# An attention and feed-forward kernel: VectorE adds one key's probabilities, six instead of seven quads of matmuls per group, a projection in two halves

## The chip, the cores and the metric

The kernel runs on one core of a Trainium2 chip. The metric is the device time of one execution in microseconds (us). The kernel before took 1667.95 us, the median of 3 runs (1665.87 to 1669.13).

Engines are called as the profile calls them: PE (TensorE, matmuls), PEld (TensorE's weight loads, which run ahead of the matmuls), DVE (VectorE), ACT (ScalarE), POOL (GpSimd) and SP (the queue that issues most DMAs).

## The reference, cut to what matters

The input `x` is 32 batches of 112 tokens with 512 features; `ctx` is 32 batches of 375 keys, of which the first 257 are image keys and the other 118 are text keys. The part in which the change lies is a cross-attention with 16 heads of 32 features:

```
q = rms_norm(linear(x, q_w, q_b), norm_q_w)                 # after a layer norm of x
k = rms_norm(linear(ctx_txt, k_w, k_b), norm_k_w);          v = linear(ctx_txt, v_w, v_b)
k_img = rms_norm(linear(ctx_img, k_img_w, k_img_b), ...);   v_img = linear(ctx_img, v_img_w, v_img_b)
img_x = attention(q, k_img, v_img)      # softmax over 257 keys
txt_x = attention(q, k, v)              # softmax over 118 keys
x = x + linear(txt_x + img_x, o_w, o_b)
```

After it, a router picks the 14 best tokens of each batch, which go through a second attention and a feed-forward layer. That second part is the same in both kernels.

## The kernel before, in words

A first phase projects the queries of all tokens. Then comes a loop over the 32 batches (`over_batches`: two are written out, 28 run in a hardware loop, two are written out), and then the second part of the network. Each engine has its own program, in an order written out by hand in a function `body(i, n, m, p)`. In batch `i` the engines also do the projections of batch `n = i + 1` and finish batch `p = i - 1`. Semaphores hold the engines together: `wait_ge(name, value)`.

The 376 key columns of a batch stand in three chunks. Chunk c (119 rows) holds the 118 text keys and, in its last row, the 257th image key; chunks a and b hold 128 image keys each. The 16 heads are handled in four groups `g` of four heads. For each group PE runs `scores_T(i, g)` (L1386, L1389: scores with keys on the partitions, in PSUM banks 2 to 5), ACT takes their exponentials into `prob[:, g % 2, c]` (`exps`, L729 for chunk c and L731 for a and b), POOL adds chunks a and b into `prob_img` (`sum_image`, L522), and PE runs `weighted_values(i, g)` (L1411). A *quad* there is four matmuls, one for each head, that write four different 32-partition parts of one bank. Seven quads make a group: `v_last`, `v_a`, `v_b` (the image values), `v_txt` (the text values), `ones_txt` (the text denominators), and, for the image denominators, `ones_last` (a matrix that has ones only in the 119th row) with chunk c and `ones_all` with `prob_img`. DVE then divides and adds (`normalise`: L995, L997, L1001).

What sets the order around the change:

- `scores_T(i, g)` writes over the banks that `exps(i, g - 1)` reads, so PE waits for `exp_done` ahead of it (ahead of `scores_T(i, 0)` it waits for DVE's `s_done` instead).
- There is one `prob_img`. POOL may write it for group g only when PE has read it for group g - 1 (`pv_full`).
- `values(n, 0)`, the projection of 128 image values of the next batch (12 matmuls, L1284 to L1286), stands between `weighted_values(i, 0)` and `scores_T(i, 2)`. It writes bank 0, so it waits until DVE has read there the projection of keys (`add_bias(n, 3)`, L969).
- `normalise(i, g)` reads what `weighted_values(i, g)` wrote; group g + 2 writes there again.
- `turn` (L1336) transposes the next batch's keys, after `exps(i, 3)` and `scale_k(n, 1..3)` (L975).
- DVE also ranks the router's scores (`ranks`, L1023 and L1025). PE waits for `rank_done` ahead of `weighted_values(i, 1)`.
- POOL's order in a batch is `inverse_rms` (L516) between the sums of groups 0 and 1 and of 1 and 2, and `residual` (L530, an addition of 112x512) between those of groups 2 and 3.

Of the kernel before, what the change touches and what calls it, by code (L numbers as in the profile page):

```python
# [6 lines left out]
ALU = mybir.AluOpType  # L7
# [5 lines left out]
B, L, D = 32, 112, 512  # L13
# [3 lines left out]
P = 128  # L17
# [30 lines left out]
def build(nc, t, out):  # L48
    with ExitStack() as ctx:
# [3 lines left out]
        def sem(name):  # L53
            return ctx.enter_context(nc.semaphore(name))
# [22 lines left out]
        def p1(name, shape, dt=F32):  # L77
            return phase1.enter_context(nc.sbuf_tensor(name, shape, dt))
# [53 lines left out]
        topT = [p1(f"topT{e}", [P, L], F32R) for e in range(2)]  # L132
        prob_img = p1("prob_img", [P, GH * L])
        p1("under_heads", [P, 672 + 1496 - GH * L + L])
        prob = p1("prob", [P, 2, 3, GH * L])
# [145 lines left out]
        top_full, topT_ready, pick_loaded, pick_ready = sem("top_full"), sem("topT_ready"), sem("pick_loaded"), sem("pick_ready")  # L281
        st_full, exp_done, img_summed = sem("st_full"), sem("exp_done"), sem("img_summed")
        pv_full, norm_step, pv_done = sem("pv_full"), sem("norm_step"), sem("pv_done")
# [197 lines left out]
        def _(pool):  # L481
# [36 lines left out]
            def sum_image(i, g):  # L518
                pool.wait_ge(exp_done, 8 * i + 2 * g + 2)
                if not isinstance(i, int) or i or g:  # L520
                    pool.wait_ge(pv_full, 4 * i + g)
                nc.gpsimd.tensor_tensor(prob_img[:], prob[:, g % 2, 1, :], prob[:, g % 2, 2, :], ALU.add).then_inc(img_summed, 1)  # L522

# [422 lines left out]
        def _(dve):  # L946
# [37 lines left out]
            def group_max(i, g):  # L984
# [5 lines left out]
                nc.vector.tensor_reduce(rows[:, :, 2 * g + 1], ps[0:L, 2:6, TAIL:CTX], AX.X, ALU.max).then_inc(s_done, 1)  # L990

            def normalise(i, g):
                dve.wait_ge(pv_full, 4 * i + g + 1)
# [101 lines left out]
            def body(i, n, m, p):  # L1095
# [14 lines left out]
                if n is not None:  # L1110
                    add_bias(n, 2)
                    scale_k(n, 1)
                if p is not None:
                    ranks(p)
                if n is not None:
                    add_bias(n, 3)
                    scale_k(n, 2)
                normalise(i, 0)
                if n is not None:
                    scale_k(n, 3)  # L1120
                normalise(i, 1)
                normalise(i, 2)
                if n is not None:
# [157 lines left out]
        def _(pe):  # L1281
# [56 lines left out]

            def values(n, k):

                cols, w, rows = ((slice(TXT, TXT + P), "v_img", P), (slice(TXT + P, CTXC), "v_img", P), (slice(0, TXT), "v", TXT))[k]
                full, done, bank, slot = value_slot(n, k)
                pe.wait_ge(done, slot)
                project(bank[0:rows], ctx_hi, ctx_lo, cols, w).then_inc(full, 1)

# [46 lines left out]
            def weighted_values(i, g, n):  # L1392
# [5 lines left out]
                if g >= 2:  # L1398
# [3 lines left out]
                sources = ((0, ((v_last, p_c, CHUNK_C), (v_a, p_a, P), (v_b, p_b, P))), (1, ((v_txt, p_c, CHUNK_C),)),  # L1402
                           (3, ((ones_txt, p_c, CHUNK_C),)), (2, ((ones_last, p_c, CHUNK_C), (ones_all, prob_img, P))))
                for slot, terms in sources:
                    for e, (left, right, rows) in enumerate(terms):
                        if right is prob_img:
                            pe.wait_ge(img_summed, 4 * i + g + 1)
                        for j in range(GH):
# [40 lines left out]
            def body(i, n, m, p):  # L1449
# [23 lines left out]
                if n is not None:  # L1473
                    values(n, 0)
                scores_T(i, 2)
                if p is not None:
                    pe.wait_ge(rank_done, i)
                weighted_values(i, 1, n)
                scores_T(i, 3)
                weighted_values(i, 2, n)  # L1480
                if n is not None:
# [210 lines left out]
```

## Time and profile before

| | us |
|---|---|
| median of 3 runs | 1667.95 |
| profiled execution, its time | 1665.81 |
| its span, first to last instruction | 1664.1 |
| PE busy (share of the span) | 1590.9 (96%) |
| PEld busy | 1245.3 (75%) |
| DVE busy | 1092.8 (66%) |
| ACT busy | 709.6 (43%) |
| POOL busy | 696.8 (42%) |

The mean granted TensorE clock is 0.98 of full speed. A row of the profile gives busy time, mean duration in ns, and the idle time of the engine just before the instructions with what ended it. Matmuls overlap each other, so their starts tell more than their durations: the time that a matmul takes from the next one is the distance between two starts. The loop is very regular: a batch takes 34.83 us, and its rows come again 34.83 us later with nearly the same distances.

### The profile page before, as it was taken

The numbers are of one execution on the slowest core, as the hardware profiler recorded it, in microseconds if no ns is written. First come the engines' busy times: TensorE is split into PE (matmuls) and PEld (weight loads), VectorE is DVE, ScalarE is ACT, GpSimd is POOL, SyncE is SP. The second block draws the span as 40 slices with busy tenths as digits, with TensorE's granted clock in tenths as the row PEclk, the third lists the DMA queues.
The fourth block names the chain that finished last, engine by engine and source line by source line (L and its number), as shares of the span: only waits on it lengthen the run. The fifth ranks groups of instructions, "written<-read, shape, count | busy, mean of one in ns | idle before, by whom it ended". The sixth has DMA issues, their size and how long they took to land.

```text
span 1664.1 us, 44189 instructions
## 1 busy us (share of the span) xinstructions
PE 1590.9 (96%) x17801; PEld 1245.3 (75%) x17801; DVE 1092.8 (66%) x1743; ACT 709.6 (43%) x1448; POOL 696.8 (42%) x775
## 2 busy tenths in 40 slices
PE   7999999999999999999999999999985899998997
PEld 5776777777777777777777777777763787777896
DVE  5754667776676766767667776777764675444775
ACT  5763444434444344443444434444332224555331
POOL 6761443444434444434434344343434680113542
PEclk9999999999999999999999999999996899999998
DMA  6841111121111221112211122111117205010000
GB/s 189 246 127 64 48 49 51 46 75 58 46 52 46 68 64 46 52 46 64 68 46 52 46 64 68 46 52 46 46 55 274 101 1 203 26 51 26 1 1 22
DMA packets 66152, 113.72 MB, mean 68 GB/s; under 512 B 21376, under 2 KB 36064, under 8 KB 64560
## 3 DMA queue, kind: packets, MB, share of 16 engines
q1 hardware_dynamic: 65264, 110.20, 20.8%
q0 software_dynamic: 832, 2.75, 0.6%
q8 instruction: 38, 0.62, 0.2%
q14 instruction: 18, 0.15, 0.0%
HBM read 82.59 MB, written 30.34 MB: 68 GB/s over the span
## 4 chain that ended last, share of the span: by engine, by line
PE 92%; DVE 3%; ACT 2%; issue 1%; POOL 1%; DMA 1%; DVEq 0%; ACTq 0%; POOLq 0%; SPq 0%
PE ps L1284 21%; PE ps L1286 18%; PE ps L1285 18%; PE ps L1411 11%; PE ps L1386 7%; PE ps L1336 3%; PE ps L1359 3%; PE ps L1563 2%; PE ps L1544 2%; PE ps L1389 2%; PE ps L1555 1%; PE ps L1318 1%; PE ps L1366 1%; PE ps L1299 1%; ACT q_row L688 0%
## 5 line engine op out<-in xcount | busy, mean ns | idle before, releaser
L995 DVE RECIPROCAL rec<-ps 128x224 f32<-128x224 f32 x128 | 199.2, 1556 | 96.5 <-PE ps L1411 93.7
L522 POOL TENSOR_TENSOR prob_img<-prob 128x448 f32<-128x448 f32 x128 | 157.2, 1228 | 236.0 <-PE ps L1411 214.8
L485 POOL TENSOR_TENSOR ctx_lo<-ctx_raw,ctx_hi 128x472 fp32r<-128x472 f32 x64 | 115.2, 1822 | 288.7 <-ACT ctx_hi L672 288.7
L729 ACT ACTIVATE prob<-ps 119x448 f32<-119x448 f32 x128 | 69.6, 544 | 249.4 <-PE ps L1389 249.4
L990 DVE TENSOR_REDUCE top<-ps 112x4 f32<-112x1028 f32 x128 | 156.3, 1221 | 0.0
L1386 PEld LDWEIGHTS ps<-q_all,k_all 32*128 32x128 f32 (+1 forms) x3072 | 121.6, 186 | 39.9 <-issue 31.7
L1386 PE MATMUL ps<-q_all,k_all 32*128 32x112 f32 (+1 forms) x3072 | 148.0, 300 | 1.4 <-ACT prob L731 1.4
L705 ACT ACTIVATE sq_junk<-proj 128x513 bf16<-128x513 f32 (+1 forms) x96 | 61.1, 636 | 184.6 <-DVE proj L969 184.6
L989 DVE TENSOR_REDUCE top<-ps 112x4 f32<-112x472 f32 x128 | 83.1, 649 | 84.8 <-PE ps L1359 84.8
L731 ACT ACTIVATE prob<-ps 128x896 f32<-128x896 f32 x128 | 116.8, 913 | 0.0
L1284 PE MATMUL ps<-w_v_img_hi,ctx_hi 128*128 128x512 f32 x256 | 107.6, 420 | 0.6
L1284 PE MATMUL ps<-w_k_img_hi,ctx_hi 128*128 128x512 f32 x256 | 107.5, 420 | 0.0
L1286 PE MATMUL ps<-w_v_img_hi,ctx_lo 128*128 128x512 f32 x256 | 101.3, 396 | 0.0
L1286 PE MATMUL ps<-w_k_img_hi,ctx_lo 128*128 128x512 f32 x256 | 101.1, 395 | 0.0
L1285 PE MATMUL ps<-w_k_img_lo,ctx_hi 128*128 128x512 f32 x256 | 101.0, 394 | 0.0
L1285 PE MATMUL ps<-w_v_img_lo,ctx_hi 128*128 128x512 f32 x256 | 100.8, 394 | 0.0
L1286 PE MATMUL ps<-hT_hi,ring_lo 128*128 128x448 f32 x224 | 83.0, 371 | 0.0
L1389 PE MATMUL ps<-topT,pick_img 32*128 32x112 f32 x1024 | 80.8, 296 | 0.0
L516 POOL TENSOR_TENSOR rstd<-sq_sum,neg_half 128x1 f32<-128x1 f32 x96 | 52.6, 548 | 56.4 <-ACT sq_junk L705 56.4
L642 POOL TENSOR_TENSOR ring_lo<-ring,wo_hi 128x512 fp32r<-128x512 f32 x16 | 20.6, 1291 | 128.2 <-ACT wo_hi L886 128.2
L1023 DVE SCALAR_TENSOR_TENSOR equal<-ps,score_now,later 112x112 f32<-112x112 f32 x32 | 10.8, 337 | 92.5 <-PE ps L1371 92.5
L1218 DVE TENSOR_REDUCE neg_top<-ps 112x1 f32<-112x112 f32 (+1 forms) x64 | 28.4, 446 | 57.9 <-PE ps L1545 57.9
(320 smaller groups left out, 4491.2 us busy)
## 6 DMA issues: line engine op xcount, KB each, us to landing
ctx_raw<-in_ctx_dram SPq DMA_DIRECT2D x32, 748.0 KB, 4.2
xh_dram<-xh SPq DMA_DIRECT2D x32, 448.0 KB, 3.1
q_dram<-q_turned SPq DMA_DIRECT2D x28, 256.0 KB, 2.8
q_all<-q_dram SPq DMA_DIRECT2D x32, 224.0 KB, 3.1
xh<-in_x_dram SPq DMA_DIRECT2D x32, 224.0 KB, 2.8
out_dram<-out_sb SPq DMA_DIRECT2D x32, 224.0 KB, 2.3
xa<-in_x_dram SPq DMA_DIRECT2D x21, 256.0 KB, 3.4
ring<-in_wq_dram SPq DMA_DIRECT2D x1, 4096.0 KB, 13.8
```

The costliest lines, as they stand in the source:

```text
L485: nc.gpsimd.tensor_tensor(ctx_lo[:, :, cols], ctx_raw[:, :, cols], ctx_hi[:, :, cols].bitcast(F32), ALU.subtract).then_inc(ctx_lo_done, 1)
L522: nc.gpsimd.tensor_tensor(prob_img[:], prob[:, g % 2, 1, :], prob[:, g % 2, 2, :], ALU.add).then_inc(img_summed, 1)
L731: nc.scalar.activation(prob[:, g % 2, 1:3, :].rearrange("p c (j q) -> p j c q", j=GH), ps[:, 2:6, L:3 * L].rearrange("p j (c q) -> p j c q ...
L989: nc.vector.tensor_reduce(rows[:, :, 2 * g], ps[0:L, 2:6, 0:TXT], AX.X, ALU.max)
L990: nc.vector.tensor_reduce(rows[:, :, 2 * g + 1], ps[0:L, 2:6, TAIL:CTX], AX.X, ALU.max).then_inc(s_done, 1)
L995: nc.vector.reciprocal(rec[:], bank[:, 2:4]).then_inc(norm_step, 1)
L1284: nc.tensor.matmul(o_, a_hi, b_hi, start=start, stop=False)
L1285: nc.tensor.matmul(o_, a_hi, b_lo, start=False, stop=False)
L1286: return nc.tensor.matmul(o_, a_lo, b_hi, start=False, stop=stop)
L1386: nc.tensor.matmul(ps[0:rows, 2 + j, out_cols], k_all[head, g, cols], q_all[head, g, :], start=True, stop=False)
L1389: last = nc.tensor.matmul(ps[0:rows, 2 + j, out_cols], pick[head, g, :], topT[g // 2][head, :], start=False, stop=True)
L1411: last = nc.tensor.matmul(ps[HD * j:HD * (j + 1), bank, slot * L:(slot + 1) * L], left[0:rows, cols], right[0:rows, L * j:L * (j + 1)], st ...
```

## The change

It does the following:

- A fourth step is put between ACT's exponentials and the image denominators. `add_tail(i, g)` on DVE waits for POOL's sum (`img_summed`) and adds `prob` of chunk c, times `ones_last`, to `prob_img` on partitions 96 to 118. `ones_last` is zero on 96 to 117 and one on 118, so only the 257th image key's row is added.
- The quad `ones_last` with chunk c is gone. The quad `ones_all` with `prob_img` now waits for `tail_added` instead of `img_summed`.
- `prob_img` has two buffers, `prob_img[:, g % 2]`. POOL's sum for group g now waits until `weighted_values` of group g - 2 is done, not g - 1. The memory comes out of the unused tile `under_heads`.
- `values(n, 0)` is cut into two halves of 6 matmuls. The first stays where it was, the second stands between `scores_T(i, 3)` and `weighted_values(i, 2)`.
- On DVE, `add_bias(n, 3)` and `scale_k(n, 2)` stand ahead of `ranks(p)` instead of behind it. `add_tail(i, 0)` stands ahead of `ranks(p)`, `add_tail(i, 1)` behind `normalise(i, 0)`, and `add_tail(i, 2)` and `add_tail(i, 3)` both behind `normalise(i, 1)`, ahead of `normalise(i, 2)`.

```diff
@@ POOL
             def sum_image(i, g):
                 pool.wait_ge(exp_done, 8 * i + 2 * g + 2)
-                if not isinstance(i, int) or i or g:
-                    pool.wait_ge(pv_full, 4 * i + g)
-                nc.gpsimd.tensor_tensor(prob_img[:], prob[:, g % 2, 1, :], prob[:, g % 2, 2, :], ALU.add).then_inc(img_summed, 1)
+                if not isinstance(i, int) or i or g >= 2:
+                    pool.wait_ge(pv_full, 4 * i + g - 1)
+                nc.gpsimd.tensor_tensor(prob_img[:, g % 2], prob[:, g % 2, 1, :], prob[:, g % 2, 2, :], ALU.add).then_inc(img_summed, 1)
@@ DVE
+            def add_tail(i, g):
+                dve.wait_ge(img_summed, 4 * i + g + 1)
+                last_rows = slice(P - HD, CHUNK_C)
+                nc.vector.scalar_tensor_tensor(prob_img[last_rows, g % 2], prob[last_rows, g % 2, 0, :], ones_last[last_rows, 0:1],
+                                               prob_img[last_rows, g % 2], ALU.mult, ALU.add).then_inc(tail_added, 1)
...
+                if n is not None:
+                    add_bias(n, 3)
+                    scale_k(n, 2)
+                add_tail(i, 0)
                 if p is not None:
                     ranks(p)
-                if n is not None:
-                    add_bias(n, 3)
-                    scale_k(n, 2)
                 normalise(i, 0)
+                add_tail(i, 1)
                 if n is not None:
                     scale_k(n, 3)
                 normalise(i, 1)
+                add_tail(i, 2)
+                add_tail(i, 3)
                 normalise(i, 2)
@@ PE
-            def values(n, k):
+            def values(n, k, chunks=range(KC)):
...
-                           (3, ((ones_txt, p_c, CHUNK_C),)), (2, ((ones_last, p_c, CHUNK_C), (ones_all, prob_img, P))))
+                           (3, ((ones_txt, p_c, CHUNK_C),)), (2, ((ones_all, prob_img[:, g % 2], P),)))
...
-                        if right is prob_img:
-                            pe.wait_ge(img_summed, 4 * i + g + 1)
+                        if slot == 2:
+                            pe.wait_ge(tail_added, 4 * i + g + 1)
...
                 weighted_values(i, 0, n)
                 if n is not None:
-                    values(n, 0)
+                    values(n, 0, range(0, 2))
                 scores_T(i, 2)
...
                 weighted_values(i, 1, n)
                 scores_T(i, 3)
+                if n is not None:
+                    values(n, 0, range(2, 4))
                 weighted_values(i, 2, n)
```

The changed file has other line numbers: L1294 to L1296 are the projections' matmuls, L1399 and L1402 the scores, L1424 the weighted values and L1346 the transposes; on DVE, L995 is `add_tail`, L1001 to L1007 `normalise` and L1029 and L1031 `ranks`.

On PE, at the end of `scores_T(i, 3)` and through `weighted_values(i, 2)` in the loop, the order before was:

```order
L1386 MATMUL ps<-q_all,k_all 128x112 x4
L1389 MATMUL ps<-topT,pick_img 128x112 x4
L1411 MATMUL ps<-prob,v_last 32x112 x4
L1411 MATMUL ps<-prob,v_a 32x112 x4
L1411 MATMUL ps<-prob,v_b 32x112 x4
L1411 MATMUL ps<-prob,v_txt 32x112 x4
L1411 MATMUL ps<-prob,ones_txt 32x112 x4
L1411 MATMUL ps<-prob,ones_last 32x112 x4
L1411 MATMUL ps<-prob_img,ones_all 32x112 x4
L1336 MATMUL ps<-ident,proj 128x118 x4
```

Now it is this, from the last three of the six projection matmuls that stand between the scores and the values:

```order
L1294 MATMUL ps<-w_v_img_hi,ctx_hi 128x512
L1295 MATMUL ps<-w_v_img_lo,ctx_hi 128x512
L1296 MATMUL ps<-w_v_img_hi,ctx_lo 128x512
L1424 MATMUL ps<-prob,v_last 32x112 x4
L1424 MATMUL ps<-prob,v_a 32x112 x4
L1424 MATMUL ps<-prob,v_b 32x112 x4
L1424 MATMUL ps<-prob,v_txt 32x112 x4
L1424 MATMUL ps<-prob,ones_txt 32x112 x4
L1424 MATMUL ps<-prob_img,ones_all 32x112 x4
L1346 MATMUL ps<-ident,proj 128x118 x4
```

Half of the projection moved in ahead of the group, and one quad of the group is gone.

On DVE, from `scale_k(n, 1)` to the start of `normalise(i, 0)` in the loop, the order before was:

```order
L975 SCALAR_TENSOR_TENSOR proj<-proj,rstd,w_txt 118x512
L1023 SCALAR_TENSOR_TENSOR equal<-ps,score_now,later 112x112
L1025 ISA
L1025 SCALAR_TENSOR_TENSOR equal,rank<-ps,score_now,equal 112x112
L968 REGISTER_ALU
L969 TENSOR_TENSOR proj<-ps,ki_bias 128x512
L974 REGISTER_ALU
L975 SCALAR_TENSOR_TENSOR proj<-proj,rstd,w_img 128x512
L995 RECIPROCAL rec<-ps 128x224
```

Now it is:

```order
L975 SCALAR_TENSOR_TENSOR proj<-proj,rstd,w_txt 118x512
L968 REGISTER_ALU
L969 TENSOR_TENSOR proj<-ps,ki_bias 128x512
L974 REGISTER_ALU
L975 SCALAR_TENSOR_TENSOR proj<-proj,rstd,w_img 128x512
L995 SCALAR_TENSOR_TENSOR prob_img<-prob,ones_last,prob_img 23x448
L1029 SCALAR_TENSOR_TENSOR equal<-ps,score_now,later 112x112
L1031 ISA
L1031 SCALAR_TENSOR_TENSOR equal,rank<-ps,score_now,equal 112x112
L1001 RECIPROCAL rec<-ps 128x224
```

The bias and the scaling of the last keys moved ahead of the ranking, and the first tail stands between them.

Later on DVE, from `normalise(i, 1)` to the start of `normalise(i, 2)`, the order before was:

```order
L995 RECIPROCAL rec<-ps 128x224
L996 REGISTER_ALU
L997 TENSOR_TENSOR o_two<-ps,rec 128x224
L998 REGISTER_ALU
L1001 TENSOR_TENSOR o_space<-o_two 128x112
L995 RECIPROCAL rec<-ps 128x224
```

Now it is:

```order
L1001 RECIPROCAL rec<-ps 128x224
L1002 REGISTER_ALU
L1003 TENSOR_TENSOR o_two<-ps,rec 128x224
L1004 REGISTER_ALU
L1007 TENSOR_TENSOR o_space<-o_two 128x112
L995 SCALAR_TENSOR_TENSOR prob_img<-prob,ones_last,prob_img 23x448 x2
L1001 RECIPROCAL rec<-ps 128x224
```

The tails of groups 2 and 3 stand there one behind the other, ahead of the next division.

## Rows read from the trace of the kernel before

**Rows 1.** The page's busy times of the engines, and the chain that ended last.

```profile
PE 1590.9 (96%) x17801; PEld 1245.3 (75%) x17801; DVE 1092.8 (66%) x1743; ACT 709.6 (43%) x1448; POOL 696.8 (42%) x775
...
PE 92%; DVE 3%; ACT 2%; issue 1%; POOL 1%; DMA 1%; DVEq 0%; ACTq 0%; POOLq 0%; SPq 0%
```

**Rows 2.** Windows: one batch, and most of the loop; the clock follows POOL.

```profile
810.00:844.83 34.83, 34.77 (x485) 26.72 (x484) 24.52 (x38) 14.89 (x30) 14.38 (x15) 1.00 0.18 55
240.00:1200.00 960.00, 958.42 (x13369) 736.82 (x13362) 676.34 (x1023) 412.37 (x803) 393.65 (x410) 1.00 0.18 54
```

**Rows 3.** Timeline of PEld in one batch: start, duration, what [idle before].

```profile
831.26 0.16 PEld L1411 LDWEIGHTS ps<-prob,v_last 119*32 119x32 f32 x8
...
832.84 0.19 PEld L1284 LDWEIGHTS ps<-w_v_img_hi,ctx_hi 128*128 128x128 f32 x1 [0.26 <-DVE proj L969]
832.95 0.19 PEld L1285 LDWEIGHTS ps<-w_v_img_lo,ctx_hi 128*128 128x128 f32 x1
...
835.28 0.19 PEld L1286 LDWEIGHTS ps<-w_v_img_hi,ctx_lo 128*128 128x128 f32 x1
835.84 0.30 PEld L1386 LDWEIGHTS ps<-q_all,k_all 32*119 32x119 f32 x8 [0.37 <-issue]
...
836.97 0.16 PEld L1411 LDWEIGHTS ps<-prob,v_last 119*32 119x32 f32 x8
837.09 0.23 PEld L1411 LDWEIGHTS ps<-prob,v_a 128*32 128x32 f32 x8
...
838.06 0.23 PEld L1411 LDWEIGHTS ps<-prob_img,ones_all 128*32 128x32 f32 x8
838.49 0.30 PEld L1386 LDWEIGHTS ps<-q_all,k_all 32*119 32x119 f32 x8 [0.20 <-ACT prob L731]
...
839.62 0.16 PEld L1411 LDWEIGHTS ps<-prob,v_last 119*32 119x32 f32 x8
...
841.21 1.26 PEld L1336 LDWEIGHTS ps<-ident,proj 118*128 118x128 f32 x12 [0.27 <-issue]
842.64 0.16 PEld L1411 LDWEIGHTS ps<-prob,v_last 119*32 119x32 f32 x8 [0.17 <-issue]
...
844.12 0.19 PEld L1284 LDWEIGHTS ps<-w_v_img_hi,ctx_hi 128*128 128x128 f32 x1 [0.17 <-issue]
```

**Rows 4.** Timeline of ACT in the same batch: the exponentials of group 2.

```profile
837.08 0.54 ACT L729 ACTIVATE prob<-ps 119x448 f32<-119x448 f32 x1 [3.46 <-PE ps L1389]
837.52 0.91 ACT L731 ACTIVATE prob<-ps 128x896 f32<-128x896 f32 x1
```

**Rows 5.** Timeline of PE: the last matmul of the keys' projection that `add_bias(n, 3)` reads.

```profile
829.57 0.40 PE L1286 MATMUL ps<-w_k_img_hi,ctx_lo 128*128 128x512 f32 x1
```

**Rows 6.** Timeline of DVE in the same batch.

```profile
826.72 1.77 DVE L975 SCALAR_TENSOR_TENSOR proj<-proj,rstd,w_txt 118x512 f32<-118x512 f32 x1 [0.24 <-POOL rstd L516]
...
832.10 0.69 DVE L969 TENSOR_TENSOR proj<-ps,ki_bias 128x512 f32<-128x512 f32 x1
832.71 0.74 DVE L975 SCALAR_TENSOR_TENSOR proj<-proj,rstd,w_img 128x512 f32<-128x512 f32 x1
...
838.60 1.56 DVE L995 RECIPROCAL rec<-ps 128x224 f32<-128x224 f32 x1 [2.28 <-PE ps L1411]
...
840.61 0.54 DVE L1001 TENSOR_TENSOR o_space<-o_two 128x112 f32<-128x112 f32 x1
...
843.26 0.27 DVE L1001 TENSOR_TENSOR o_space<-o_two 128x112 f32<-128x112 f32 x1
```

**Rows 7.** Timeline of POOL in the same batch.

```profile
826.65 1.29 POOL L526 TENSOR_TENSOR out_sb<-xh 112x512 f32<-112x512 f32 x1
...
832.93 1.53 POOL L522 TENSOR_TENSOR prob_img<-prob 128x448 f32<-128x448 f32 x1 [2.74 <-PE ps L1411]
...
838.64 1.13 POOL L522 TENSOR_TENSOR prob_img<-prob 128x448 f32<-128x448 f32 x1 [3.67 <-PE ps L1411]
839.73 1.29 POOL L530 TENSOR_TENSOR xh<-xh,out_bias 112x512 f32<-112x512 f32 x1
```

More of the change, by code:

```diff
@@ L132, in build @@
         topT = [p1(f"topT{e}", [P, L], F32R) for e in range(2)]
-        prob_img = p1("prob_img", [P, GH * L])
-        p1("under_heads", [P, 672 + 1496 - GH * L + L])
+        prob_img = p1("prob_img", [P, 2, GH * L])
+        p1("under_heads", [P, 672 + 1496 - 2 * GH * L + L])
         prob = p1("prob", [P, 2, 3, GH * L])
@@ L281, in build @@
         top_full, topT_ready, pick_loaded, pick_ready = sem("top_full"), sem("topT_ready"), sem("pick_loaded"), sem("pick_ready")
-        st_full, exp_done, img_summed = sem("st_full"), sem("exp_done"), sem("img_summed")
+        st_full, exp_done, img_summed, tail_added = sem("st_full"), sem("exp_done"), sem("img_summed"), sem("tail_added")
         pv_full, norm_step, pv_done = sem("pv_full"), sem("norm_step"), sem("pv_done")
@@ L1112, in body @@
                     scale_k(n, 1)
-                if p is not None:
-                    ranks(p)
                 if n is not None:
@@ L1117, in body @@
                     scale_k(n, 2)
+                add_tail(i, 0)
+                if p is not None:
+                    ranks(p)
                 normalise(i, 0)
+                add_tail(i, 1)
                 if n is not None:
@@ L1337, in turn @@
                 last.then_inc(turned, 1)
-            def values(n, k):
+            def values(n, k, chunks=range(KC)):
                 cols, w, rows = ((slice(TXT, TXT + P), "v_img", P), (slice(TXT + P, CTXC), "v_img", P), (slice(0, TXT), "v", TXT))[k]
                 full, done, bank, slot = value_slot(n, k)
-                pe.wait_ge(done, slot)
-                project(bank[0:rows], ctx_hi, ctx_lo, cols, w).then_inc(full, 1)
+                if 0 in chunks:
+                    pe.wait_ge(done, slot)
+                last = project(bank[0:rows], ctx_hi, ctx_lo, cols, w, chunks)
+                if KC - 1 in chunks:
+                    last.then_inc(full, 1)
             def output(i):
```

## The prediction

> **What bounds the kernel now.** I read the page's busy times and its chain first: PE is busy for 96% of the span and makes up 92% of the chain that ended last [rows 1]. The windows then say that this is even truer inside the loop: in one batch of 34.83 us PE is busy for 34.77 us, and over 960 us of the loop for 958.42 us, at a granted clock of 1.00, so 2.4 GHz throughout [rows 2]. Every other engine has 10 us or more to spare in a batch. So the time of the loop is the length of PE's list, plus the places where PE waits. Those places are small, and "busy" hides them because matmuls overlap. The timeline of the weight loads shows them: the reader should look at the distances between starts, and at the bracket in front of each part [rows 3]. I then followed ACT, DVE and POOL through the same batch [rows 4, 6, 7], because the change puts one more engine between the exponentials and PE's last quad.
>
> **The quad that goes.** From v_a (837.09) to ones_all (838.06) are five quads, 0.97 us, so one is 0.194 us [rows 3]. There are 32 batches of 4 groups; a batch would gain 4 x 0.194 = 0.78 us if PE had nothing else to wait for. Group by group:
>
> - Group 0: the quad is gone in full, 0.19 us. Behind it the projection of the values starts after an idle time of 0.26 us that DVE's add_bias ended, where the same change of work behind group 3 costs 0.17 us [rows 3]. With add_bias ahead of the ranking, it starts when the keys' last matmul is done (829.57 + 0.40, about 830.0 [rows 5]) and ends 2 us before it is needed. That gives another 0.09 us.
> - Group 1: nothing. scores_T(3) waits for ACT to read scores_T(2): the bracket says so [rows 3]. The loads of scores_T(2) start at 835.84, its exponentials end at 837.52 + 0.91 = 838.43 [rows 4], and scores_T(3) starts at 838.49. These 2.65 us are set by ACT, whatever stands between. Group 1 was a cover of almost the same length (838.06 + 0.23 + 0.17 = 838.46). Without a quad it is 0.19 us shorter, and PE waits these 0.19 us.
> - Group 2: 0.19 us, and the transposes behind it no longer start late. They come 0.27 us after the last load, against 0.17 us elsewhere [rows 3]; I take the 0.10 us for the wait for the last exponentials, which the moved half of the projection now covers.
> - Group 3: 0.19 us.
>
> **The projection in halves.** The work is the same, 12 matmuls. From the second load (832.95) to the twelfth (835.28) are ten steps of 0.233 us. The whole piece, 832.84 to 835.84, is 3.00 us, so 12 x 0.233 = 2.80 us and 0.20 us for entering and leaving it [rows 3]. Two halves pay this twice: 6 x 0.233 + 0.20 = 1.60 us each, 0.20 us more in a batch. The trace has no direct switch scores, half, values; from below the second switch could be free (0), from above it could be all of the 0.37 us bracket [rows 3]. I take 0.20, the nearest row's own remainder. The shorter first half also removes cover from scores_T(2), which waits for the exponentials of group 1; before it had over 3 us to spare there and now has 1.6 us.
>
> The Trainium skill ("TensorEngine Tiling (Array Packing)", Key Properties) says that changing the tiling mode drains TensorE. By that rule each of the two halves has to pay for the drain, which speaks against the split; the 0.20 us above is where the trace agrees.
>
> **The sum for PE.** 0.19 + 0.09 (group 0) + 0.19 + 0.10 (group 2) + 0.19 (group 3) - 0.20 = 0.56 us a batch. Laid out as a timeline from 831.26: half at 832.56, scores_T(2) at 834.16, scores_T(3) at 836.81, second half at 837.95, group 2 at 839.55, transposes at 840.84, group 3 at 842.27, next values at 843.57 instead of 844.12: 0.55 us. I take 0.55 us.
>
> **DVE's new step: is it in time?** add_tail reads two tensors in SBUF and is 23x448. Nearest rows: the same operation at 128x512 takes 0.74 us, an addition at 128x112 0.27 us [rows 6]. On a line between them 448 columns take 0.67 us; the bounds are 0.27 and, if POOL is in its way, 1.77 us. It costs PE nothing as long as it ends before the sixth quad, 0.90 us after a group's second load. The work that hides it:
>
> - Group 0: add_bias 830.00, scale_k 830.61 (spacing of the rows 832.10 and 832.71), add_tail 831.3 to 832.0. Needed at 832.16. That is about 0.1 us to spare, the tightest one that does not hang on a race. An overrun costs what it overruns.
> - Group 1: the sixth quad is due at 836.2. DVE ranks until 832.8, normalises group 0 for 2.3 us (838.60 to 840.61 and 0.27 [rows 6]), adds the tail until 835.8: 0.4 us to spare. Behind it wait scale_k(3) and, through it, only the transposes at 840.8.
> - Group 2: the sum can only start when the exponentials end at 836.75, is 1.13 us long, and POOL's residual of 1.29 us follows directly, until 839.2 [rows 7]. DVE's normalise(1) ends in the addition to o_space, which waits for the residual exactly as before (0.54 instead of 0.27 us, ended 0.13 us after the residual did [rows 6, 7]): until 839.35. add_tail(2) runs from there to 840.0, and is needed at 840.45.
> - Group 3: sum from 839.5, held up by add_tail(2) to 841.1, tail to 841.8, needed at 843.2. normalise(2), queued behind it, starts 0.8 us late, and normalise(3) ends at 846.5, where it ended before; the next batch's first maxima need DVE at 847.1.
>
> The two-buffer prob_img is worth nothing by itself (POOL waited without holding up PE) but lets the sum start right behind ACT, which all of the above uses. The load of the next q is issued after scores_T(3), which comes no later relative to its user. Nothing outside the loop changes. In the last batch, which has no projections, PE waits for exponentials anyway; I count it as zero.
>
> 31 x 0.55 = 17 us. Against the profiled execution's own 1665.81 us (span 1664.1) this gives 1648.8; the median of the runs is 2.1 us above that execution, so 1651 us.
>
> **Rivals.**
>
> *A, slower: POOL wins the race behind group 2.* DVE and POOL do not read SBUF side by side in two-tensor operations. scale_k(1) took 1.77 instead of 0.74 us beside POOL's out_sb and ended 0.55 us after it; a sum that met scale_k took 1.53 instead of 1.13 us [rows 6, 7]. So whoever of add_tail(2) and sum(3) starts first goes first. I have add_tail(2) ready at 839.35 and sum(3) at 839.4 to 839.5 (exponentials of group 3 end 2.59 us behind the start of their scores, as those of group 2 do, at 836.81 + 2.59, and POOL follows 0.05 to 0.1 us later). If POOL is first, it ends at about 840.6 and add_tail(2) at 841.2 instead of 840.0, against 840.45: PE waits 0.75 us in each batch. Net 0.20 us worse, 31 times: 1668 + 6 = 1674 us. It decides from 0.1 us on. For it: the margin is that small. Against it: both are tied to the same residual, and DVE, queued right behind it, has nothing to wait for.
> The Trainium skill ("GPSIMD Engine Reference", the table of its key facts) gives the interface as shared, with contention for Vector instructions with two SBUF inputs; the rows agree. And "VectorE: DVE Perf Modes", section "Two Vector instructions with no wait between them", states that an instruction whose inputs start in another quadrant of partitions than the last one's is held until that has finished. 
>
> *B, a smaller gain: tails that come a little late.* If add_tail(0) or (2) costs PE 0.1 to 0.4 us in every batch without the race being lost, for example because an add_tail takes 0.9 us, a batch gains 0.3 us: 1668 - 9 = 1659 us. For it: 0.1 us of room at group 0. Against it: the operation has fewer columns than the 0.74 us row.
>
> *C, a larger gain.* If the second switch is free and ACT's 2.65 us shrink, because POOL and DVE now work at other times, a batch gains up to 0.97 us (all four quads, 0.09, 0.10 and no switch): 1638 us at most; I price this case at 0.75 us, 1645 us. Against it: the exponentials read PSUM, and their 1.35 us (837.08 to 838.43 [rows 4]) is work that the change does not touch.
>
> **How the numbers follow.** Forecast 1651 us with a chance of 0.62 (own range 1647 to 1656), B 0.14, C 0.09, A 0.12, and 0.03 for something between A and B that is no change. A measurement of this kernel can tell about 0.2%, 3.3 us, from no change. Faster by more than that: 0.62 + 0.14 + 0.09 = 0.85. Within it: 0.03. Slower: 0.12. The range of 1643 to 1664 holds the forecast, B and nearly all of C and leaves out A.
>
> **What would show it.** A batch's period of 34.28 us; matmul groups of six quads, 0.194 us apart; the load of scores_T(3) still 2.65 us behind that of scores_T(2), with a longer wait for ACT (some 0.4 us in the bracket); no wait for DVE's proj ahead of the values; add_tail of about 0.65 us, the one of group 2 ahead of POOL's sum of group 3, and that sum lengthened by it. I am wrong if PE shows a wait for prob_img ahead of ones_all, above all in group 2 with the sum of group 3 at its normal 1.13 us (A), or in group 0 (B), or if the second half costs more than 1.6 us.

## The result, and the profile after

| | before | after |
|---|---|---|
| median, same chip, 4 runs each | 1666.91 us | 1652.14 us (1651.32 to 1654.16) |
| ratio, 95% interval | 1 | 0.9914 [0.9896, 0.9932] |
| profiled execution, its span | 1665.81, 1664.1 us | 1652.05, 1650.3 us |
| one batch in the loop | 34.83 us | 34.27 us |

The changed kernel is 0.9% faster, 1652.1 us against the 1651 us of the forecast. The page's busy times and chain answer to [rows 1]:

```profile
PE 1569.6 (95%) x16777; PEld 1219.0 (74%) x16777; DVE 1188.0 (72%) x1871; ACT 706.1 (43%) x1448; POOL 700.7 (42%) x775
...
PE 88%; ACT 5%; DVE 3%; issue 1%; POOL 1%; DMA 1%; SPq 0%; DVEq 0%; ACTq 0%; POOLq 0%
```

PE has 1024 matmuls less (128 quads, each of which the profile counts as 8), DVE 128 instructions more. DVE's 95 us more cost nothing in the loop (no_tail below). ACT's share of the chain rose because scores_T(3) now really waits for it: in the batch at 802 us the chain runs through the exponentials of group 2, and in the batch at 810 us of the kernel before it stayed on PE. The windows of the batch and of the loop answer to [rows 2]: PE is still never idle for long, again at a granted clock of 1.00.

```profile
802.05:836.32 34.27, 34.12 (x453) 25.89 (x453) 27.57 (x42) 14.79 (x29) 14.45 (x15) 1.00 0.18 56
240.00:1200.00 960.00, 955.66 (x12631) 725.55 (x12631) 771.87 (x1151) 414.52 (x814) 405.41 (x421) 1.00 0.18 55
```

The timeline of the weight loads of that batch answers to [rows 3]; 821.04 here is 831.26 there. Columns as there: start, duration, what, [idle before].

```profile
802.05 0.18 PEld L1372 LDWEIGHTS ps<-k_hi,q_hi 32*112 32x112 f32 x4 [0.36 <-issue]
...
821.04 0.16 PEld L1424 LDWEIGHTS ps<-prob,v_last 119*32 119x32 f32 x8
...
821.93 0.23 PEld L1424 LDWEIGHTS ps<-prob_img,ones_all 128*32 128x32 f32 x8
822.34 0.19 PEld L1294 LDWEIGHTS ps<-w_v_img_hi,ctx_hi 128*128 128x128 f32 x1 [0.17 <-issue]
...
823.93 0.30 PEld L1399 LDWEIGHTS ps<-q_all,k_all 32*119 32x119 f32 x8 [0.36 <-issue]
...
825.06 0.16 PEld L1424 LDWEIGHTS ps<-prob,v_last 119*32 119x32 f32 x8
...
825.96 0.23 PEld L1424 LDWEIGHTS ps<-prob_img,ones_all 128*32 128x32 f32 x8
826.58 0.30 PEld L1399 LDWEIGHTS ps<-q_all,k_all 32*119 32x119 f32 x8 [0.40 <-ACT prob L731]
...
827.72 0.19 PEld L1294 LDWEIGHTS ps<-w_v_img_hi,ctx_hi 128*128 128x128 f32 x1
...
829.31 0.16 PEld L1424 LDWEIGHTS ps<-prob,v_last 119*32 119x32 f32 x8 [0.37 <-ACT prob L731]
...
830.21 0.23 PEld L1424 LDWEIGHTS ps<-prob_img,ones_all 128*32 128x32 f32 x8
830.61 1.26 PEld L1346 LDWEIGHTS ps<-ident,proj 118*128 118x128 f32 x12 [0.17 <-issue]
```

Three things are to be seen. No `prob_img` row has a bracket, so no tail came late; from the first batch to the last but one PE waits for a tail only once, 0.17 us in the first. The wait for DVE's `proj` ahead of the values is gone (0.17 instead of 0.26 us), and so is the late start of the transposes (0.17 instead of 0.27 us). Scores_T(2) to scores_T(3) is 826.58 - 823.93 = 2.65 us as before, with the idle time ahead of the latter grown from 0.20 to 0.40 us.

The timelines of DVE and POOL show the race of group 2; the rows answer to [rows 6, 7].

```profile
819.78 0.69 DVE L969 TENSOR_TENSOR proj<-ps,ki_bias 128x512 f32<-128x512 f32 x1 [1.53 <-PE ps L1296]
...
821.17 0.69 DVE L995 SCALAR_TENSOR_TENSOR prob_img<-prob,ones_last,prob_img 23x448 f32<-23x448 f32 x1
...
828.51 0.69 DVE L1007 TENSOR_TENSOR o_space<-o_two 128x112 f32<-128x112 f32 x1
829.24 0.68 DVE L995 SCALAR_TENSOR_TENSOR prob_img<-prob,ones_last,prob_img 23x448 f32<-23x448 f32 x1
```

```profile
827.78 1.30 POOL L530 TENSOR_TENSOR xh<-xh,out_bias 112x512 f32<-112x512 f32 x1
829.34 1.58 POOL L522 TENSOR_TENSOR prob_img<-prob 128x448 f32<-128x448 f32 x1 [0.26 <-ACT prob L731]
```

DVE's tail starts at 829.24, 0.10 us ahead of POOL's sum, and keeps its 0.68 us; the sum takes 1.58 instead of 1.13 us.

### The profile page after: what moved, and what is told of

It reads as the page before. It is cut to its first block, busy times and chain, and to the rows that moved or that the text cites. A ratio compares the mean times of both kernels' runs of the same rounds, so it can differ in the third digit from the quotient of the medians.

```text
span 1650.3 us, 42268 instructions
## 1 busy us (share of the span) xinstructions
PE 1569.6 (95%) x16777; PEld 1219.0 (74%) x16777; DVE 1188.0 (72%) x1871; ACT 706.1 (43%) x1448; POOL 700.7 (42%) x775
## 4 chain that ended last, share of the span: by engine, by line
PE 88%; ACT 5%; DVE 3%; issue 1%; POOL 1%; DMA 1%; SPq 0%; DVEq 0%; ACTq 0%; POOLq 0%
PE ps L1294 21%; PE ps L1295 18%; PE ps L1296 18%; PE ps L1424 7%; PE ps L1399 7%; PE ps L1372 3%; PE ps L1346 3%; PE ps L1578 2%; ACT prob L731 2%; PE ps L1402 2%; PE ps L1559 2%; PE ps L1570 1%; ACT prob L729 1%; PE ps L1328 1%; PE ps L1379 1%
## 5 line engine op out<-in xcount | busy, mean ns | idle before, releaser
L1001 DVE RECIPROCAL rec<-ps 128x224 f32<-128x224 f32 x128 | 199.0, 1555 | 7.1 <-PE ps L1424 3.4
L1399 PEld LDWEIGHTS ps<-q_all,k_all 32*128 32x128 f32 (+1 forms) x3072 | 121.6, 186 | 45.9 <-issue 32.0
L1399 PE MATMUL ps<-q_all,k_all 32*128 32x112 f32 (+1 forms) x3072 | 148.0, 300 | 6.2 <-ACT prob L731 6.2
L995 DVE SCALAR_TENSOR_TENSOR prob_img<-prob,ones_last,prob_img 23x448 f32<-23x448 f32 x128 | 87.5, 684 | 40.0 <-POOL prob_img L522 37.0
L1294 PE MATMUL ps<-w_v_img_hi,ctx_hi 128*128 128x512 f32 x256 | 110.7, 432 | 0.0
L1294 PE MATMUL ps<-w_k_img_hi,ctx_hi 128*128 128x512 f32 x256 | 107.4, 419 | 0.0
L1296 PE MATMUL ps<-w_v_img_hi,ctx_lo 128*128 128x512 f32 x256 | 101.2, 395 | 0.0
L1296 PE MATMUL ps<-w_k_img_hi,ctx_lo 128*128 128x512 f32 x256 | 101.1, 395 | 0.0
L1296 PE MATMUL ps<-hT_hi,ring_lo 128*128 128x448 f32 x224 | 83.1, 371 | 0.0
L969 DVE TENSOR_TENSOR proj<-ps,ki_bias 128x512 f32<-128x512 f32 x64 | 44.3, 693 | 51.0 <-PE ps L1296 51.0
L1402 PE MATMUL ps<-topT,pick_img 32*128 32x112 f32 x1024 | 80.8, 296 | 0.0
```

The costliest lines, as they stand in the source:

```text
L995: nc.vector.scalar_tensor_tensor(prob_img[last_rows, g % 2], prob[last_rows, g % 2, 0, :], ones_last[last_rows, 0:1], prob_img[last_rows, ...
L1001: nc.vector.reciprocal(rec[:], bank[:, 2:4]).then_inc(norm_step, 1)
L1294: nc.tensor.matmul(o_, a_hi, b_hi, start=start, stop=False)
L1296: return nc.tensor.matmul(o_, a_lo, b_hi, start=False, stop=stop)
L1399: nc.tensor.matmul(ps[0:rows, 2 + j, out_cols], k_all[head, g, cols], q_all[head, g, :], start=True, stop=False)
L1402: last = nc.tensor.matmul(ps[0:rows, 2 + j, out_cols], pick[head, g, :], topT[g // 2][head, :], start=False, stop=True)
```

## The experiments

Each is the changed kernel with one edit. Ratios are against the kernel before on the same chip. The period of a batch is read between two starts of `k_hi,q_hi` in the profiled execution.

| kernel | us, median | ratio, 95% interval | batch, us |
|---|---|---|---|
| after | 1652.14 | 0.9914 [0.9896, 0.9932] | 34.27 |
| no_tail | 1650.25 | 0.9892 [0.9875, 0.9908] | 34.26 |
| one_buffer | 1659.23 | 0.9937 [0.9920, 0.9954] | 34.41 |
| turn_moved | 1642.16 | 0.9849 [0.9828, 0.9870] | 34.02 |
| bias_back | 1706.61 | 1.0226 [1.0210, 1.0242] | 36.13 |
| no_split | 1685.76 | 1.0112 [1.0095, 1.0129] | 35.33 |
| op_ahead | 1674.85 | 1.0039 [1.0024, 1.0053] | 35.03 |
| op_behind | 1651.86 | 0.9904 [0.9887, 0.9920] | 34.26 |
| op_ahead_residual_early | 1652.63 | 0.9910 [0.9894, 0.9927] | 34.27 |
| turn_moved_again | 1646.04 | 0.9859 [0.9841, 0.9877] | 34.02 |
| seven_at_end | 1642.65 | 0.9848 [0.9835, 0.9861] | 34.02 |

**no_tail: does DVE's new step cost anything?**

```diff
-                add_tail(i, 0)   # and the calls for 1, 2 and 3
-                            pe.wait_ge(tail_added, 4 * i + g + 1)
+                            pe.wait_ge(img_summed, 4 * i + g + 1)
```

> Leaves add_tail out and lets PE wait for POOL's sum: the 257th image key is missing from the image denominators. Theory (the tails are hidden, with 0.07 to 0.35 us to spare): period 34.27 us as in the changed kernel, 1652 us. Rival (the tails, or their waits, cost PE something): a shorter period; 0.1 us a tail would be 33.9 us and 1640 us.

Measured: 34.26 us a batch, within 0.01 us of after. All four tails are hidden in the loop. The medians are 1.9 us apart with overlapping intervals. The traces differ in the last batch: from its fourth scores to the transposed router scores no_tail takes 33.07 us and after 35.62 us. These are the weight loads of after there:

```profile
1237.03 0.16 PEld L1424 LDWEIGHTS ps<-prob_img,ones_all 128*32 128x32 f32 x8 [0.53 <-DVE prob_img L995]
...
1240.56 0.16 PEld L1424 LDWEIGHTS ps<-prob_img,ones_all 128*32 128x32 f32 x8 [1.14 <-DVE prob_img L995]
...
1242.28 0.16 PEld L1424 LDWEIGHTS ps<-prob_img,ones_all 128*32 128x32 f32 x8 [0.57 <-DVE prob_img L995]
```

With no projections beside it, the last batch has no cover: PE waits 0.53 + 1.14 + 0.57 = 2.24 us for tails. no_tail has none of these brackets, and its stretch is 2.55 us shorter.

**one_buffer: what is the second sum buffer worth?**

```diff
-                    pool.wait_ge(pv_full, 4 * i + g - 1)
-                nc.gpsimd.tensor_tensor(prob_img[:, g % 2], ...
+                    pool.wait_ge(pv_full, 4 * i + g)
+                nc.gpsimd.tensor_tensor(prob_img[:, 0], ...
...
+    # add_tail and the ones_all quad use prob_img[:, 0] too
```

> One prob_img instead of two; POOL's sum waits again until the group before has been weighed. Theory (two buffers are worth nearly nothing by themselves): sums 0 to 2 start as before the edit within 0.2 us; sum 3 starts 1.2 us later, its tail ends at about the time it is needed, and normalise(2) behind it starts 1 us later: period 34.3 to 34.5 us, 1652 to 1659 us. Rival (the second buffer carries the gain): the period returns to 34.8 us or more, 1667 us or more.

Measured: 34.41 us and 1659.2 us, about 7 us behind after; only about 31 x 0.14 = 4.3 us of it is the batch. Another 1.6 us lie in the last batch: from its fourth scores to the transposed router scores one_buffer takes 37.25 us and after 35.62 us, and PE's waits for tails there are 3.69 instead of 2.24 us. Its first batch also starts 2.7 us later (153.22 against 150.51 us), ahead of everything that the edit touches, and so does op_ahead's (153.15 us); that part is not put down to the buffer. The timelines of POOL and then DVE in one_buffer show group 3:

```profile
733.07 1.15 POOL L522 TENSOR_TENSOR prob_img<-prob 128x448 f32<-128x448 f32 x1 [1.71 <-PE ps L1424]
```

```profile
734.25 0.68 DVE L995 SCALAR_TENSOR_TENSOR prob_img<-prob,ones_last,prob_img 23x448 f32<-23x448 f32 x1 [2.04 <-POOL prob_img L522]
```

The sum waits for PE's group 2 and not for ACT, and the last tail waits 2.04 us for it instead of 1.04. The normalisations queued behind it end later. Behind them, in the next batch, DVE splits the attention's output (`oT_lo`, L1011), and PE's output projection waits for that (PEld, start to start 3.48 us):

```profile
707.52 0.18 PEld L1372 LDWEIGHTS ps<-k_hi,q_hi 32*112 32x112 f32 x4 [0.37 <-DVE top L990]
708.02 0.17 PEld L1294 LDWEIGHTS ps<-w_o_hi,oT_hi 128*112 128x112 f32 x1 [0.33 <-issue]
...
711.00 0.18 PEld L1372 LDWEIGHTS ps<-k_hi,q_hi 32*112 32x112 f32 x4 [0.38 <-issue]
```

In after this distance is 3.33 us, with 0.18 us of idle time ahead of the output projection instead of 0.33; the 0.15 us are the whole loss of a batch. `oT_lo` ends at 707.91, 0.11 us ahead of the projection's first load; in after it ends 0.79 us ahead. The bracket of the scores at 707.52 names the router maxima, but it is no longer than in after (0.37 against 0.38 us). No tail holds PE up. So the second buffer is worth 0.14 us a batch through DVE's end, and some 1.6 us in the last batch.

**bias_back: what is the earlier add_bias worth?**

```diff
-                if n is not None:
-                    add_bias(n, 3)
-                    scale_k(n, 2)
                 add_tail(i, 0)
                 if p is not None:
                     ranks(p)
+                if n is not None:
+                    add_bias(n, 3)
+                    scale_k(n, 2)
```

> On DVE the tail of group 0, then the ranking, then add_bias(3) and scale_k(2): only the move of the bias is undone. Theory: the first half of the values waits 0.1 us for add_bias again (a wait for DVE's proj comes back), perhaps 0.05 us more for the tail of group 1; period 34.4 us, 1655 to 1657 us. Rival (the 0.09 us of the prediction were no wait): period 34.27 us, 1652 us.

Measured: 1706.6 us, some 50 us more than expected. The direction was right and the size was not. Weight loads of PEld in one batch of bias_back:

```profile
712.02 0.19 PEld L1294 LDWEIGHTS ps<-w_v_img_hi,ctx_hi 128*128 128x128 f32 x1 [0.45 <-DVE proj L969]
...
716.42 0.16 PEld L1424 LDWEIGHTS ps<-prob_img,ones_all 128*32 128x32 f32 x8 [0.74 <-DVE prob_img L995]
...
721.55 0.16 PEld L1424 LDWEIGHTS ps<-prob_img,ones_all 128*32 128x32 f32 x8 [1.14 <-DVE prob_img L995]
```

And DVE and POOL in the batch after it:

```profile
748.01 1.56 DVE L975 SCALAR_TENSOR_TENSOR proj<-proj,rstd,w_img 128x512 f32<-128x512 f32 x1
...
752.52 1.66 DVE L975 SCALAR_TENSOR_TENSOR proj<-proj,rstd,w_img 128x512 f32<-128x512 f32 x1
...
756.11 0.80 DVE L1007 TENSOR_TENSOR o_space<-o_two 128x112 f32<-128x112 f32 x1
```

```profile
747.88 1.14 POOL L522 TENSOR_TENSOR prob_img<-prob 128x448 f32<-128x448 f32 x1 [2.36 <-ACT prob L731]
...
752.50 1.13 POOL L522 TENSOR_TENSOR prob_img<-prob 128x448 f32<-128x448 f32 x1 [2.52 <-ACT prob L731]
753.60 1.74 POOL L530 TENSOR_TENSOR xh<-xh,out_bias 112x512 f32<-112x512 f32 x1
755.63 1.15 POOL L522 TENSOR_TENSOR prob_img<-prob 128x448 f32<-128x448 f32 x1 [0.29 <-ACT prob L731]
```

add_bias costs PE its own 0.28 us (0.45 against 0.17). But behind the ranking scale_k(2) also starts 0.13 us after POOL's sum of group 1 and takes 1.56 instead of 0.74 us. Normalise(0) and tail(1) come late (0.74 us for PE), scale_k(3) runs into the sum of group 2 (0.02 us behind it, 1.66 us), and tail(2) is no longer ahead of the sum of group 3 (1.14 us). 0.28 + 0.74 + 1.14 = 2.16 us. The second of them stands in front of scores_T(3) and replaces its wait for ACT, whose bracket falls from 0.40 to 0.17 us. That leaves 1.93 us, against a period that grew by 1.86 us.

**no_split: is the moved half the cover of tail(2)?**

```diff
-                    values(n, 0, range(0, 2))
+                    values(n, 0)
...
-                if n is not None:
-                    values(n, 0, range(2, 4))
```

> The projection of the first image values stands whole behind weighted_values(0) again; all else as in the changed kernel. Theory (the second half is the cover of the longer way to ones_all): one change of work less on PE, 0.18 us, but group 2 now starts 1.6 us earlier than the tail of group 2 can be there; its ones_all waits 1.3 us for prob_img: period 34.27 + 1.2 = 35.4 us, about 1687 us. Rival (the split only covers the exponentials of group 3, 0.2 us, for which it pays 0.2 us): period 34.3 us, 1652 us.

Measured: 1685.8 us, 35.33 us a batch. The row of group 2 in PEld's timeline of no_split:

```profile
746.89 0.16 PEld L1424 LDWEIGHTS ps<-prob_img,ones_all 128*32 128x32 f32 x8 [1.31 <-DVE prob_img L995]
```

Without the half in front of group 2, PE waits 1.31 us for tail(2). The split is what makes the tail free: it costs one switch of 0.18 us and saves this wait. Without it the whole change is slower than the kernel before (1.0112).

**op_ahead and op_behind: who wins the race, and what does losing it cost?** A memset of DVE takes 0.17 us and is needed by no one. It is put once ahead of tail(2), and once behind it.

```diff
+        idle_tile = p1("under_heads", ...)
...
                 normalise(i, 1)
+                nc.vector.memset(idle_tile[:, 0:128], 0.0)   # op_ahead
                 add_tail(i, 2)
+                nc.vector.memset(idle_tile[:, 0:128], 0.0)   # op_behind
                 add_tail(i, 3)
```

> Adds one small DVE operation that computes nothing (a memset of 128 columns, 0.1 to 0.2 us) ahead of the tail of group 2. Theory (race): the tail now starts behind POOL's sum of group 3, which had started 0.10 us after it, and is held until the sum ends: it lasts 1.5 us or more, ones_all of group 2 waits 0.8 us, period 35.1 us, 1677 us. Rival (plain slack): the tail had 0.29 us to spare and uses 0.1 to 0.2 of it: period 34.27 us, 1652 us.

> Adds the same DVE operation between the tails of groups 2 and 3, where DVE waits 1.0 us for POOL. Theory and rival both: period 34.27 us, 1652 us. It shows that the operation itself costs nothing.

op_ahead, timelines of DVE, POOL and PEld around group 2:

```profile
740.12 0.70 DVE L1007 TENSOR_TENSOR o_space<-o_two 128x112 f32<-128x112 f32 x1
740.79 0.17 DVE L1130 MEMSET under_heads<- 128x128 f32 x1
740.97 2.21 DVE L995 SCALAR_TENSOR_TENSOR prob_img<-prob,ones_last,prob_img 23x448 f32<-23x448 f32 x2
```

```profile
740.94 1.15 POOL L522 TENSOR_TENSOR prob_img<-prob 128x448 f32<-128x448 f32 x1 [0.26 <-ACT prob L731]
```

```profile
742.62 0.16 PEld L1425 LDWEIGHTS ps<-prob_img,ones_all 128*32 128x32 f32 x8 [0.79 <-DVE prob_img L995]
```

POOL's sum starts 0.03 us ahead of the tail and keeps its 1.15 us; the tail (the first of the two in the row) lasts up to 1.61 us, the longest of L995's 128. PE waits 0.79 us. 34.27 + 0.79 = 35.06 us, measured 35.03. In op_behind the same memset costs nothing, 34.26 us a batch and 1651.86 us. So it is not DVE's load but the order of the two starts.

**op_ahead_residual_early: the memset stays, the residual goes.** POOL's `residual(i)` moves from behind the sum of group 2 to behind the sum of group 1.

```diff
                 sum_image(i, 1)
...
+                residual(i)
...
                 inverse_rms(n, 3)
                 sum_image(i, 2)
-                residual(i)
                 sum_image(i, 3)
```

> The operation ahead of the tail of group 2 again, but POOL's residual stands between its sum of group 1 and inverse_rms(3), where POOL waits 2.7 us for ACT. Theory (race): the addition to o_space is no longer held up, the tail starts 0.3 us before the sum of group 3 in spite of the added operation, and PE waits for neither: period 34.3 us, 1652 us. Rival (the added DVE time itself is what costs): as in the run without the move, 35.1 us.

DVE in this kernel, and POOL's sum of group 3:

```profile
760.23 0.28 DVE L1007 TENSOR_TENSOR o_space<-o_two 128x112 f32<-128x112 f32 x1
760.48 0.17 DVE L1130 MEMSET under_heads<- 128x128 f32 x1
760.66 0.69 DVE L995 SCALAR_TENSOR_TENSOR prob_img<-prob,ones_last,prob_img 23x448 f32<-23x448 f32 x1
```

```profile
761.06 1.29 POOL L522 TENSOR_TENSOR prob_img<-prob 128x448 f32<-128x448 f32 x1 [1.51 <-ACT prob L731]
```

The o_space addition takes 0.28 instead of 0.70 us. These 0.42 us outweigh the memset's 0.17, the tail is first again by 0.40 us, and the batch is back at 34.27 us. It is the residual that pushes DVE to the edge of the race, as the prediction had it.

**turn_moved: is there free room behind group 1?** The prediction says that group 1 gains nothing because scores_T(3) waits for ACT. Then work put there should be free. The transpose of the router's scores (`turn_score`, a block of its own between others) goes there; it stood ahead of group 0. It writes another PSUM region, DVE's ranking moves between tail(2) and tail(3), and tail(0) goes ahead of add_bias. PE's wait for `rank_done` moves behind weighted_values(3), the one for `topT_ready` goes, and one for bank 1 comes in.

```diff
-        score_row = ps[0:L, 7, 2 * L:3 * L]
+        score_row = ps[0:L, 1, 0:L]
...
-                    turn_score(p)            # ahead of weighted_values(i, 0)
                 weighted_values(i, 1, n)
+                if p is not None:
...
+                    turn_score(p)
                 scores_T(i, 3)
```

> The router scores' transpose (0.23 us of PE) leaves its place ahead of weighted_values(0) and stands between weighted_values(1) and scores_T(3), where PE waits 0.22 us for ACT; it writes bank 1, and the ranking moves into DVE's idle time of 1.04 us between the tails of groups 2 and 3. Theory (PE's list, with the distance of 2.65 us between scores_T(2) and scores_T(3) set by ACT): the transpose costs nothing there, period 34.27 - 0.23 = 34.04 us, about 1645 us. Rival (the bracket of 0.40 us ahead of scores_T(3) is the normal change of work and no wait): period 34.27 us, 1652 us. A tail that now comes late would show as a wait for prob_img ahead of ones_all.

Measured: 34.02 us a batch and 1642.2 us, 10 us better than after. The batches make up 31 x 0.25 = 7.8 us of it; the same kernel measured again was 1646.0 us, 6 us better than after. Weight loads in turn_moved:

```profile
717.50 0.30 PEld L1399 LDWEIGHTS ps<-q_all,k_all 32*119 32x119 f32 x8 [0.37 <-issue]
...
718.63 0.16 PEld L1424 LDWEIGHTS ps<-prob,v_last 119*32 119x32 f32 x8
...
719.92 0.13 PEld L1384 LDWEIGHTS ps<-ident,score_now 112*112 112x112 f32 x1 [0.17 <-issue]
720.16 0.30 PEld L1399 LDWEIGHTS ps<-q_all,k_all 32*119 32x119 f32 x8
```

720.16 - 717.50 = 2.66 us, with the transpose between them: it is free there. This shows that the distance is not set by what stands between, and in after the bracket names ACT. The freed quad of group 1 makes the room: with the seventh quad group 1 ended 0.03 us ahead of scores_T(3) in the prediction's rows, and the transpose needs 0.23 us. The transpose there with seven quads was not run.

**turn_moved_again and seven_at_end: the last batch.** turn_moved once more, and beside it a version that goes back to seven quads and no tails in the last batch only.

```diff
-                add_tail(i, g)
+                if n is not None:
+                    add_tail(i, g)
...
+    # last batch: (ones_last, p_c, CHUNK_C) again, waits for img_summed
```

> The kernel of turn_moved once more, to stand beside the next one on the same chip: period 34.02 us, 1642 us.

> turn_moved, but the last batch, which has no projections to cover the tails, keeps seven quads and leaves DVE's tails out. Theory (the tails cost nothing in the loop and about 2 us of PE's waits in the last batch, where they were counted as zero): no wait for DVE's prob_img in the last batch, which gets 1 to 1.5 us shorter; 1640.5 to 1641.5 us. Rival (what the last batch loses in waits for the tails is given back behind them): no difference in time.

From the last batch's fourth scores to the transposed router scores: 35.45 us in turn_moved, 35.65 us in turn_moved_again, 33.12 us in seven_at_end. So some 2.4 us come back in the trace, as in no_tail, where 1 to 1.5 us were expected. The clock does not explain them: granted over the stretch it is 0.74, 0.74 and 0.71. The medians don't settle it: 1642.16, 1646.04 and 1642.65 us, where 1640.5 to 1641.5 us were expected of the last. turn_moved and turn_moved_again are one kernel, and they show why. From the transposed router scores to the first transposes of the gathered tokens, behind the loop (PEld, first turn_moved, then the same kernel again):

```profile
1250.82 0.17 PEld L1384 LDWEIGHTS ps<-ident,score_now 112*112 112x112 f32 x1 [5.74 <-issue]
...
1269.56 2.90 PEld L1526 LDWEIGHTS ps<-ident,normed 112*128 112x128 f32 x16 [10.72 <-DVE normed L1163]
```

```profile
1251.58 0.17 PEld L1384 LDWEIGHTS ps<-ident,score_now 112*112 112x112 f32 x1 [5.75 <-issue]
...
1272.44 2.90 PEld L1526 LDWEIGHTS ps<-ident,normed 112*128 112x128 f32 x16 [12.18 <-DVE normed L1163]
```

That is 18.74 against 20.86 us, for one and the same kernel. The stretch holds the gather of the chosen tokens by DMA. Over all kernels it lies between 18.6 us (before) and 21.1 us; what sets it stays open. Both versions, at 0.985 to 0.986 of the kernel before, beat after.

## Why the prediction was right

1. **The quad** (0.194 us, three of four groups gain): right. (821.93 - 821.04) is four steps and the v_last load, 0.89 us, where five steps and that load took 1.09 us before. All four groups are one quad shorter, and groups 0, 2 and 3 gain by it.
2. **Group 1 gains nothing**: right, 2.65 us before and after; shown by turn_moved. The prediction's "Every other engine has 10 us or more to spare in a batch" holds for DVE, ACT and POOL; PEld has 34.83 - 26.72 = 8.1 us, and nothing hangs on it.
3. **add_bias ahead of the ranking, 0.09 us**: right as a term of PE's list. What bias_back shows beyond it was not seen: the order also keeps scale_k(2) and everything behind it out of POOL's way. With the tails in place it is worth 1.86 us a batch and not 0.09.
4. **Two halves, 0.20 us for the second switch**: the halves take 823.93 - 822.34 = 1.59 us and 829.31 - 827.72 = 1.59 us, 3.18 against 3.00 us. 0.18 us, so the nearest row's remainder was the right choice between 0 and 0.37. The Trainium skill ("TensorEngine Tiling (Array Packing)", Key Properties) says that a change of the tiling mode drains TensorE; the trace agrees, each half pays for entering and leaving. What the split is worth beside it, the 1.31 us that no_split waits, stands in the prediction only as the time by which tail(2) is needed, and not as a term.
5. **The tails in time**: right in the loop. A tail takes 0.684 us (forecast 0.67). Tail(0) ends at 821.86 and is needed at 821.93, 0.07 us to spare where 0.1 was forecast; that it costs nothing is shown by no_tail. The tail starts 0.04 us after its predecessor's end, where scale_k(2) starts 0.08 us before it. The Trainium skill ("VectorE: DVE Perf Modes", "Two Vector instructions with no wait between them") states that an instruction whose inputs start in another quadrant of partitions than the last one's is held until the earlier ones have finished; these rows fit, about 0.1 us a tail, but no run here changes the quadrant alone. One slip of words: the 0.90 us to the sixth quad count from a group's first load, not its second; the prediction's times use the first, and they came out.
6. **The race of rival A**: the margin of 0.1 us was right, and so was the price. In op_ahead DVE loses it: a wait of 0.79 us (forecast 0.75) and 1674.85 us (forecast 1674). The rival's mechanism is real; in this kernel DVE wins, by a margin that the prediction had only as a bound (0.05 to 0.15 us against a threshold of 0.1).
7. **Two buffers worth nothing by themselves**: the working named only POOL's wait. one_buffer shows 0.14 us a batch, through normalise(3) and the `oT_lo` that PE's output projection waits for, and 1.6 us in the last batch. That is some 6 of the 15 us, so this term was wrong for the last batch and small but not nothing in the loop.
8. **The sum**: 34.28 us forecast, 34.27 measured. The last batch's scores start at 1230.10 us before and 1213.20 us after, 16.9 us earlier, where 31 x 0.55 = 17 us was forecast.
9. **"In the last batch ... I count it as zero"** is the term that was wrong, though its two parts nearly cancel. The tails cost 2.55 us there (35.62 against 33.07 us in no_tail). Without tails the stretch is 2.0 us shorter than before (35.08 us). The saved quads are not needed for that: seven_at_end has seven quads in the last batch, no tails, and takes 33.12 us. The second buffer is what the rows point to: POOL's sum of group 1 starts 11.91 us behind the fourth scores in before, where it waits for PE, and 10.19 us behind them in no_tail and after, where it waits for ACT; and one_buffer is 1.6 us longer there than after. It was not isolated without tails. The net is 0.54 us (35.08 to 35.62 us), at a granted clock of 0.73 over the stretch in both kernels.
10. **"Nothing outside the loop changes"**: the gather stretch took 2.22 us more in this execution (18.60 to 20.82). Since one kernel (turn_moved) shows both lengths, it is not put down to the change; with a single trace of the kernel before it can't be excluded either. 16.90 - 0.54 - 2.22 = 14.14 us, against 13.8 us by which the spans differ; the other 0.34 us lie behind the gather (371.11 against 371.45 us) and were not followed.
11. **The last 1.1 us** between 1651 and 1652.14 us are partly luck. The loop came out within 0.2 us, but 2.1 us were put on for the distance of one execution from the median, and the four executions of the kernel before lie 4.8 us apart. The profiled execution itself was forecast at 1648.8 us and took 1652.05.

Rivals B and C fell: no tail comes late in the loop behind its first batch, the second switch costs 0.18 us and is not free, and ACT's 2.65 us did not shrink.

## What to carry to other kernels

When a step is added between two engines, list for each consumer how long the work in front of it lasts, and look at the first and last round of the loop apart: there the cover is missing. Where two engines' instructions exclude each other and start within 0.1 us of each other, price the lost race and keep every short instruction off the front of the one that must win. A forced wait is room: where an engine waits for another anyway, independent work is free, and here that added 0.25 us a batch, 6 to 10 us in the medians, to the change's 15.

## What the runs showed of the hardware

- Two-tensor operations of DVE and of POOL on SBUF don't run side by side, one is held until the other has almost ended: 0.74 became 1.56 or 1.66 us on DVE, 1.13 became 1.58 us on POOL, and the one that started first kept its time in every row shown. A lead of 0.02 to 0.13 us decided it.
- One such hold can cascade: in bias_back two DVE operations put behind the ranking became three waits in a batch, 54 us in all (1706.6 against 1652.1).
- A memset of 0.17 us that no one waits for cost 1674.85 - 1652.14 = 23 us ahead of tail(2), and nothing behind it (1651.86 us).
